# Making GpSimd wait until nearly all of its queued indirect transfers have been executed

## The reference

```
h = relu(layernorm(x));  w = act(edge_attr @ Wfc1) @ Wfc2
msg = products of w, f(h)[idx] and the edge's direction      # one row per edge
x = x + combine(segment_sum(msg, key, N_nodes), h)           # layer 0 divides by the count
```

## Time and profile before

| what | value |
|---|---|
| device time without the profiler, median of 3 runs | 9685.46 us (9671.8 to 9688.35) |
| the profiled execution: time from first to last instruction (its span) | 12324.9 us |
| POOL busy in it | 7006.2 us, 57% |
| PE, DVE, ACT busy in it | 7174.4, 7264.9, 4965.0 us |
| indirect transfers | 7,040: 1,664 and 416 scatters, 1,248 sends in layer 0, 3,712 gathers |

### The profile page before, as it was taken

One profiled execution on the slowest core, in us unless ns is written; L12 is line 12 of the kernel. 1 busy time (PEld: TensorE's weight loads), 2 busy tenths in 40 slices (PEclk: granted clock), 3 DMA queues, 4 the chain that ended last, 5 costly groups with the idle time before them and its releaser, 6 DMA issues. The chain is left out here.

```text
span 12324.9 us, 170670 instructions
## 1 busy us (share of the span) xinstructions
PE 7174.4 (58%) x31166; PEld 4913.0 (40%) x31166; DVE 7264.9 (59%) x21188; ACT 4965.0 (40%) x16490; POOL 7006.2 (57%) x7069
## 2 busy tenths in 40 slices
PE   4444444444545545455555555577677777777778
PEld 3222222222222222222222222255566777677668
DVE  6444444444555555555655555566566666676665
ACT  2333333333333333333333333333455555555554
POOL 3555555556666666666665666555555555555551
PEclk7555555556777777777777777778788888888889
DMA  2222222223333333333333334444444444444457
GB/s 80 72 71 71 73 72 72 71 72 107 108 111 109 111 108 110 108 108 111 111 109 106 112 108 110 99 136 136 117 119 121 121 119 118 121 121 121 119 116 185
DMA packets 826473, 1315.62 MB, mean 107 GB/s; under 512 B 228520, under 2 KB 627624, under 8 KB 826280
## 3 DMA queue, kind: packets, MB, share of 16 engines
q0 software_dynamic: 337920, 667.48, 19.7%
q1 hardware_dynamic: 417496, 547.30, 14.7%
q10 hardware_dynamic: 70992, 100.14, 2.3%
HBM read 862.45 MB, written 914.08 MB: 144 GB/s over the span
## 5 line engine op out<-in xcount | busy, mean ns | idle before, releaser
L1445 POOL DMA_INDIRECT feat_m<-feat_tab,rows_m x3712 | 3704.0, 998 | 2622.5 <-issue 1195.9
L1545 PE MATMUL pair<-prod_m,hot_m 128*128 128x160 f32 x14848 | 2479.6, 331 | 906.1 <-DVE prod_m L1751 845.7
L1545 PEld LDWEIGHTS pair<-prod_m,hot_m 128*128 128x128 f32 x14848 | 2360.3, 215 | 1025.3 <-issue 830.8
L1522 PE MATMUL bank<-prod_m,hot_m 128*128 128x449 f32 x2476 | 1409.4, 703 | 1964.1 <-DVE prod_m L1788 1191.8
L1578 ACT ACTIVATE prod_m<-part_m,rows_m 128x64 f32<-128x64 f32 x5568 | 1431.4, 337 | 2783.0 <-issue 1347.7
L1566 ACT ACTIVATE hot_m<-hot_m,rows_m 128x128 f32<-128x128 f32 x5568 | 1728.6, 389 | 1675.9 <-DVE hot_m L1734 1345.5
L1809 DVE SCALAR_TENSOR_TENSOR acc_m<-acc_m,same_block,pair 128x640 f32<-128x640 f32 (+1 forms) x1237 | 1025.1, 829 | 2191.9 <-remote 1673.8
L652 POOL DMA_INDIRECT sorted_rows<-rows_e,place_e x1664 | 1602.4, 963 | 1124.5 <-ACT place_e L687 622.4
L1464 POOL DMA_INDIRECT sorted_rows<-later_m,place_m x1248 | 1281.1, 1027 | 848.3 <-ACT place_m L1626 496.6
L1522 PEld LDWEIGHTS bank<-prod_m,hot_m 128*128 128x128 f32 x2476 | 537.0, 238 | 2777.2 <-issue 2682.6
L478 PE MATMUL pair<-fc,hT_e 64*128 64x192 f32 x3328 | 632.9, 544 | 1277.6 <-ACT rows_e L681 1240.6
(11 more groups left out here) (250 smaller groups left out, 9521.6 us busy)
## 6 DMA issues: line engine op xcount, KB each, us to landing
agg_tab<-acc_m ACTq DMA_DIRECT2D x928, 320.0 KB
rows_m<-sorted_rows SPq DMA_DIRECT2D x928, 229.0 KB
agg_tab<-acc_m ACTq DMA_DIRECT2D x928, 224.5 KB
rows_m<-sorted_rows SPq DMA_DIRECT2D x928, 197.0 KB
feat_m<-feat_tab,rows_m POOLq DMA_INDIRECT x3712
turned_m<-in_turned ACTq DMA_DIRECT2D x159, 256.0 KB
agg_s<-agg_tab SPq DMA_DIRECT2D x98, 320.0 KB, 3.6
sorted_rows<-rows_e,place_e POOLq DMA_INDIRECT x1664
```

Source lines behind the costliest of these rows:

```text
L1445: pool.indirect_dma_start(out=feat[s % RING][:, k, :], out_offset=None, in_=g.feat_tab[l.n], in_offset=bass.IndirectOffsetOnAxis(ap=rows[s ...
L1522: mm = pe.matmul(out[:, 0, :], hot[s % l.hot_bufs][:, k, 0, :], prod[s % prods][:, k, 0:l.agg], start=(k == 0), stop=(k == ST_TILES - 1))
L1545: mm = pe.matmul(dst, hot[s % l.hot_bufs][:, k, q, :], rhs, start=(k == 0 and col == 0), stop=(k == ST_TILES - 1), skip_group_check=True)
```

## The change

Each of the three places where POOL issues indirect transfers gives them a second semaphore (`engine_sem`), which POOL itself raises when it has executed the transfer's issue; it does not wait for the data to land. The code then waits on it:

- scatters of `sort_edges` and `middle`: ahead of the first and of the fifth of the eight, until all but two of those before have been executed (`QUEUED` = 4, `LEFT` = 2). So at most six can stand passed on and not executed.
- gathers of `messages`: ahead of each pair, until all earlier gathers but one have been executed; where two scatters of `send` stand between the last pair and this one, until all earlier gathers have been executed, so that these two scatters are what is left. Scatters of `send` don't count.

```diff
+QUEUED, LEFT = 4, 2
...
+        scattered = sem("scattered")
...
                 pool.wait_ge(copied, c + 1)
                 pool.wait_ge(evicted, c * 4 + 4)
                 pool.wait_ge(r.place_here, c + 1)
-                settle(pool, g.passed)
                 for k in range(CHUNK_TILES):
+                    if k % QUEUED == 0:
+                        if step is None or step * CHUNK_TILES + k >= QUEUED:
+                            pool.wait_ge(scattered, c * CHUNK_TILES + (k - LEFT))
+                        settle(pool, g.passed)
                     pool.indirect_dma_start(
                         out=g.sorted_rows[0], out_offset=bass.IndirectOffsetOnAxis(ap=place[s][:, k:k + 1], axis=0),
-                        in_=rows[s][:, k, :], in_offset=None).then_inc(rows_sent[s], 16)
+                        in_=rows[s][:, k, :], in_offset=None, engine_sem=scattered).then_inc(rows_sent[s], 16)
...
                 if step is None or step >= RING:
                     pool.wait_ge(prod_ready, u - RING + 1)
+                if step is None or step >= 2:
+                    pool.wait_ge(gathered, u * ST_TILES - (0 if sends and WINDOW[(s - 1) % TURN][1] >= 2 else 1))
                 settle(pool, g.passed)
                 for k in range(ST_TILES):
                     pool.indirect_dma_start(
                         out=feat[s % RING][:, k, :], out_offset=None, in_=g.feat_tab[l.n],
-                        in_offset=bass.IndirectOffsetOnAxis(ap=rows[s % HELD][:, k, l.idx_at:l.idx_at + 1], axis=0)
-                    ).then_inc(feat_here[s % RING], 16)
+                        in_offset=bass.IndirectOffsetOnAxis(ap=rows[s % HELD][:, k, l.idx_at:l.idx_at + 1], axis=0),
+                        engine_sem=gathered).then_inc(feat_here[s % RING], 16)
```

More of the change, by code:

```diff
@@ L1080, in send @@
                 pool.wait_ge(r.place_here, c + 1)
-                settle(pool, g.passed)
                 for k in range(CHUNK_TILES):
+                    if k % QUEUED == 0:
+                        if step is None or step * CHUNK_TILES + k >= QUEUED:
+                            pool.wait_ge(scattered, c * CHUNK_TILES + (k - LEFT))
+                        settle(pool, g.passed)
                     pool.indirect_dma_start(
                         out=g.sorted_rows[1], out_offset=bass.IndirectOffsetOnAxis(ap=place[s][:, k:k + 1], axis=0),
-                        in_=later[s][:, k, :], in_offset=None).then_inc(sent[s], 16)
+                        in_=later[s][:, k, :], in_offset=None, engine_sem=scattered).then_inc(sent[s], 16)
             turns(pool, MID, 2, send)
@@ L1366, in messages @@
         acc_stored = [sem(f"acc_stored{s}") for s in range(l.accs)]
-        hot_ready, hot_scaled, prod_ready, sum_ready, acc_ready, iota_made = (
-            sem(x) for x in ("hot_ready", "hot_scaled", "prod_ready", "sum_ready", "acc_ready", "iota_made"))
+        hot_ready, hot_scaled, prod_ready, sum_ready, acc_ready, iota_made, gathered = (
+            sem(x) for x in ("hot_ready", "hot_scaled", "prod_ready", "sum_ready", "acc_ready", "iota_made", "gathered"))
         if sends:
```

## The result

| | before | after |
|---|---|---|
| device time, median of 13 runs each | 9,684.17 us (9,671.80 to 9,698.14) | 9,705.51 us (9,684.88 to 9,715.16) |
| ratio, with 95% interval | | 1.0021 (1.0014 to 1.0029) |
| span of the profiled execution | 12,324.9 us; recorded again 9,660.5 | 9,713.4 us |

What follows compares the result with a forecast made beforehand. POOL's issue of indirect transfers was taken to bound the kernel: 9,543 us least time, plus 142 above it in timed runs, plus 0 for waits, marks and gain, made 9,685 us; whole range 9,420 to 9,880.

Steps and rivals of the forecast that it cites:

- the forecast of no difference: Whole kernel: no difference that can be told, under 0.2% or about 19 us; 9,685 us, chance 0.42.
- the likeliest case: Whole kernel: waits, marks and gain each 0 us; 9,685 us, own range 9,666 to 9,705.
- the one on the waits: POOL's new waits in stages 1, 3 and messages: the transfers left cover each restart, so 0 us; uncovered, 0.50 us each.
- the third rival: Gathers of messages: mark over 0.75 us late empties POOL's queue; 9,840 us for layer 0, 10,210 for both; chance 0.15.
- The fourth rival: All transfers: marks and waits cost 0.004 to 0.02 us per transfer; 9,705 to 9,800 us, chance 0.11.
- The first rival: POOL's idle stalls (one of 6.06 us) are in timed runs too, from its queue: 8,595 to 9,400 us, chance 0.13.
- The sign that was set for it: Profiled span: near 12,300 us if recording makes the stalls; falling by up to 1,400 us if the queue does.
- The argument from the sum: POOL, whole kernel: 7,040 transfers and gaps, 9,111 us, plus 432 outside make 9,543; 2,782 us idle belong to the profile alone.
- The rule against the change: POOL's dispatch: its cores overlap successive instructions, which waiting on completion gives up; cost only where too little is queued.
- The 142 us above POOL's least time: Timed median less POOL's 9,543 us: stage 4 alone can hold it, with POOL, PE and DVE equally loaded.

Runs made afterwards that it cites:

- the first recording: The kernel before, unchanged, as first profiled: span 12,324.9 us, against a median of 9,685.46 us in the timed runs.
- Marks alone: Kernel before plus the second semaphore on all 5,792 transfers, without new waits or the second settle of a chunk: 0.9994, 9,672.58 us.
- 518 waits with two left: The change in the scatters of sort_edges and middle only, gathers as in the kernel before: 0.9996 against the kernel before, 9,672.59 us.
- 1,852 waits of the gathers: The whole change, but two gathers left where the change leaves one: 1.0006 against the kernel before.
- the second recording: The kernel before, unchanged, profiled once more: 9,662.35 us, span 9,660.5 us.
- the kernel with none left: The changed kernel with LEFT = 0 and waits until all earlier gathers are executed: 1.0911 against the kernel before, 10,564.98 us.
- 156 settles: The whole change with two more settle instructions per pair of gathers: 1.0025 against the kernel before.

## Why the prediction was wrong

The time came out 20 us above the forecast of no difference, which had 0.42; slower had 0.26. The whole range, 9,420 to 9,880, held it, which says little of a loss of 20 us; the likeliest case's own, 9,666 to 9,705, missed it by 0.5 us.

*The step that failed* is the one on the waits: "Where one gather is left, it is due at T + 0.30 + 0.95 + 0.30 = T + 1.55: 0.75 us to spare ... So no wait shows: 0 us." Its numbers hold for the wait that it describes: ahead of the first gathers of pairs the gap is 0.30 us, and with no cover a wait costs 0.52 us. But it took for granted that the sequencer, once released, passes on transfer after transfer. It stops for 2.5 us about once in a hundred, and then one gather does not cover it. That term was taken as 0 and measured 20 us in the time (22 by the gaps). Some 2 us of these come from a smaller slip in the same step: "elsewhere in layer 0 it is two scatters" does not hold for four of its first steps, where nothing is left and the step's own price, 0.50 us, shows. The pause could have been read beforehand: the gaps of 2.06 us ahead of second gathers stand in the first recording, most of them charged to nothing, at a fixed distance of 104 transfers; I took them for more of the same stalls. That the wait comes too late where one gather is left was the third rival, with another mechanism (a late mark) and at every wait instead of one in 52 of layer 1. The mark is not late: `settle` runs at 7153.9, and the issue that it waits for ends at 7153.89.

*The fourth rival had the size,* 9,705 us at its lower end, and not the reason: it charged marks and waits by the piece. Marks alone are 0.9994, 518 waits with two left are 0.9996, 1,852 waits of the gathers 1.0006 with two left.

*The first rival fell.* The stops of 6 us are, with the same long queues, neither in the second recording, whose span fits the timed runs, nor in that with marks alone. The sign that was set for it misled: a falling span was to tell of the queue, and the span fell, but it falls as much for the kernel before, recorded again. The argument from the sum (7,040 transfers x 1.27 us against the median) was right against the rows of the stalls. (The rival's own time has a slip: 1,411 of 12,324.9 us is 1,109 of 9,685, not 1,090, which makes 8,576 us; nothing hangs on it.) What disturbed the first recording stays open. The Trainium skill, NOTIFIC - the notification-queue block, section 7.1, has as one of three behaviours of a full record queue that it holds up what writes to it; the runs show only that the same kernel, recorded again, was not held up.

*The rule against the change,* the Trainium skill, GPSIMD Engine Reference, section 2.1, was weighed rightly as the case of too short a queue. With something left there is no overlap to lose (0.30 us stays 0.30); with nothing left the gap grows to 0.82 us.

*The 142 us above POOL's least time* were laid on stage 4 alone. In the second recording stage 3 holds as much: its 416 transfers at 1.265 us need 526 of 639 us (6,330.59 to 6,969.68), 113 us too many, and stage 4's 1,856 at 1.25 us 2,320 of 2,437, 117. Together that is more than 142, in part because the sum's 6,999.1 us of transfers came from the disturbed recording; in the second they take 6,927.6. That changed nothing in the forecast.

## What to carry to other kernels

A queue ahead of an engine covers the stops of whoever fills it, also rare ones that no profile shows as long as they are covered: before bounding it, leave room for the longest stop, not for the ordinary step. Here two queued gathers do, one does not. And a span that is 27% above the timed median is a recording to take again before its idle time is explained.

## What the runs showed of the hardware that was not expected

POOL's sequencer pauses 2.5 us while it passes on indirect transfers, every 104 transfers in layer 1 of this kernel, whether 52 or 156 settles lie between and whether these take 134 or 166 us. It can be seen only where the sequencer's own instructions are close around the transfers. In stage 1 of the kernel with none left they come every 96 transfers; from the start of one of its gaps to the start of the next (1230.86 and 1366.39):

```profile
L657 POOL DMA_INDIRECT sorted_rows<-rows_e,place_e x96: 955/961/1057, 1230.9 to 1363.6; - x96
```

So the distance is not the same for the scatters of stage 1 and the gathers of layer 1. What the sequencer does in that time no run tells.

In stage 1 nearly one issue in 32 takes 1.24 us instead of 0.96. It stands beside two bf16 instructions of DVE:

```profile
991.08 0.42 DVE L368 TENSOR_TENSOR same_e<-hi_e 128x256 bf16 x1
991.11 1.24 POOL L657 DMA_INDIRECT sorted_rows<-rows_e,place_e  x1 [0.30 <-DMA sorted_rows<-rows_e,place_e]
...
991.54 0.29 DVE L378 TENSOR_TENSOR below_e<-same_e,tri 128x256 bf16<-128x256 bf16 x1
```

It goes with the order in which the two begin. In after, 46 issues run beside an L368 that began 0.01 to 0.09 us ahead of them, and each takes 1.16 us or more; the five beside one that began with them or later take 0.96. (In the second recording of before one of 51 does not fit.) The kernel before has them as well (52 issues over 1.2 us in stage 1, against 47), so they are no part of the difference. The Trainium skill, SBUF - State Buffer, section SBUF: two separate sides, has DVE and POOL share a pair of ports, which whichever begins first keeps for its whole instruction, if DVE's has two inputs in SBUF and POOL's reads SBUF. The order in these rows agrees; that this is the cause here was not tried.
